# Delta rounds: the key scale folded into other operations, POOL's scaling of keys taken out

## The chip, the cores and the metric

One core of a Trainium2 chip runs the whole program in one launch. The time is device microseconds from start to end. Five engines matter: TensorE (PE in the profile, its weight loads PEld), VectorE (DVE), ScalarE (ACT), GpSimd (POOL), and SyncE (SP), which issues most transfers. Each engine works through its own instructions in order; they meet only through semaphores. All data are 32-bit floats.

## What is computed

The program is a stack of four blocks on an input of 4 x 512 x 512: a gated scan, a mixture of experts, a gated delta rule with 16 heads of 128, and a second mixture. The change touches only the delta rule, whose inner step is, in the reference:

```python
q = silu(q).reshape(B, S, NH, D)
k = silu(k).reshape(B, S, NH, D) * D ** (-0.5)
v = silu(v).reshape(B, S, NH, D)
def step(St, inp):
    q_, k_, v_, a_, b_ = inp
    sk = einsum('bhij,bhj->bhi', St, k_)
    err = sk - v_
    Sn = a_[..., None, None] * St - b_[..., None, None] * err[..., None] * k_[..., None, :]
    o_ = einsum('bhij,bhj->bhi', Sn, q_)
    return (Sn, o_)
```

After it the output is normalised per head, scaled by `ln_w`, shifted by `ln_b` and multiplied by a gate, `sigmoid(x @ Wg)`.

## The kernel before, in words

`phase_delta` handles 16 rounds (`NR`), one for each pair of a group of four heads and a sequence of 512 tokens. Round 0 and round 15 are written apart; rounds 1 to 14 are a loop of seven passes with two rounds in each. A round has four chunks (`TPB`) of 128 tokens. The recurrence over a chunk is turned into matrices: `kk` = k k^T, `kq` = k q^T, a decay matrix `G`, `negL` = -kk * G, whose unit triangular inverse `R` is needed, and `A` = kq * G. After the inverses come four sequential steps in which the state `S` goes from chunk to chunk.

Each round `r` also prepares round `r + 1`: twelve projections ("units": k 0 to 3, q 4 to 7, v 8 to 11), each a matmul on PE (L1564), a first tap on ACT (L1776), three more taps on DVE (L1929) and a SiLU on ACT (L1781). Units share the two PSUM banks `pj`, so that unit u + 2 can only be projected once DVE has done the taps of unit u (L1562); unit 7 has a bank of its own.

The orders are written out by hand, one for each engine.

- **POOL** (L1519 to L1532): the masks `masked_la` and `masked_b` of chunks 1 to 3 (L1487, L1491); then `scale_keys` (L1493), four instructions for the four heads of the next round's keys, each of which waits for the SiLU of that head; then `finish_gates` (L1505), which turns tanh into sigmoid on this round's four gate chunks; then `gate_out` (L1507), twelve instructions that apply `ln_w`, `ln_b` and the gate to the output of round r - 1, chunk by chunk (L1517); last `copy_tables` and the masks of chunk 0 for the next round.
- **DVE** (L2010): for each chunk `G`, `negL`, `A`, `kd` (L2016 to L2024) and taps of a unit; then `diagonal_inverse` (L1932), which inverts the 32 x 32 diagonal blocks in 31 steps, each a product `block_t` (L1946) and a sum `block_X` (L1950), both `tensor_tensor` with both inputs and the output in SBUF and each waiting for the one before it. Taps of unit 3 stand before step 24 and those of unit 4 before step 27. Two transposes follow (L1952, L1954), then taps of units 5 and 6.
- **ACT** (L1802): tanh of the gate chunks (L1768), with the SiLUs of keys 0 to 2 and the normalisation of the previous output's chunks 0 to 2 (L1797) between them; then the first taps of units 3 and 4, the SiLU of key 3, the first tap of unit 5, the normalisation of chunk 3; then it waits for the first transpose and spreads the blocks into `T` and `R` (L1848).
- **PE** (L1588): the round begins with a wait for `k_scaled` (L1598). After the chunk matrices come the gate projections (L1577), units 3 to 6 and the first half of unit 7, then `z_blocks` (L1645), which waits for the spread `T`, the second half of unit 7, `r_blocks` (L1659), further steps of the inverse, and the state steps with units 8 to 11 between them. The turned-out output of round r - 1 (L1585) waits for `gate_out`.

Of the kernel before, what the change touches and what calls it, by code (L numbers as in the profile page):

```python
# [19 lines left out]
P = 128  # L20
# [20 lines left out]
DH = 128  # L41
HG = 4
# [8 lines left out]
class Program:  # L51
# [8 lines left out]
    def sem(self, name):  # L60

        self.phase_sems.append(self.nc.alloc_semaphore(name=name))
        return self.phase_sems[-1]
# [55 lines left out]
def stand(e, passed):  # L119

    e.sem_inc(passed, 1)
# [1166 lines left out]
def phase_delta(pr, con, tab):  # L1288
# [3 lines left out]
    H4 = [P, HG, P]  # L1292
    NR = NG * NB
    TAP_STEPS = TAPS - 1
    CONVS = 3 * HG
    NL = len(LEVELS)
    NM = TPB * HG
# [5 lines left out]
    with ExitStack() as st:  # L1303
        sb = lambda n, s: pr.sb(st, "c_" + n, s)
        ps = lambda n, s: pr.ps(st, "c_ps_" + n, s)
        sem = lambda n: pr.sem("c_" + n)
# [4 lines left out]
        heads = [{m: sb(f"{m}T{i}", [P, HG, SEQ]) for m in "kq"} for i in range(2)]  # L1311
# [5 lines left out]
        beta, log_decay, before, upto, whole = (sb(k, [P, TPB, HG]) for k in ("beta", "log_decay", "before", "upto", "whole"))  # L1317
        masked_la, masked_b = sb("masked_la", [P, HG, P]), sb("masked_b", [P, HG, P])
        G = sb("G", [P, 2, HG, P])
        negL = sb("negL", [P, TPB, HG, P])  # L1320
        A = sb("A", [P, TPB, HG, P])
        R, T = sb("R", [P, TPB, HG, P]), sb("T", [P, TPB, HG, P])
        Z = sb("Z", [P, TPB, HG, P])
        kd = sb("kd", [P, TPB - 1, HG, DH])
# [19 lines left out]
        kk, kq, d4, z4, r4, t4 = (by_head(x) for x in (kk_ps, kq_ps, d_ps, z_ps, r_ps, t_ps))  # L1344
# [20 lines left out]
        tables = sem("tables")  # L1365
# [1 line left out]
        tap_done = sem("tap_done")  # L1367
        conv_step = sem("conv_step")
        silu_done = sem("silu_done")
        k_scaled = sem("k_scaled")  # L1370
        g_copied, g_done = sem("g_copied"), sem("g_done")
        la_masked, b_masked = sem("la_masked"), sem("b_masked")
        d_ready, decay_done, G_done = sem("d_ready"), sem("decay_done"), sem("G_done")
        kk_ready, L_done, A_done = sem("kk_ready"), sem("L_done"), sem("A_done")
# [4 lines left out]
        kt_ready, kd_done, vt_ready, v_done = sem("kt_ready"), sem("kd_done"), sem("vt_ready"), sem("v_done")  # L1379
# [28 lines left out]
        def _(e):  # L1408
# [21 lines left out]
            for r in range(NR):  # L1430
# [6 lines left out]
                if r + 2 < NR:  # L1437
                    e.wait_ge(gp_ready, TPB * r + TPB)
                    e.wait_ge(conv_step, TAP_STEPS * (CONVS * (r + 1) + 2))
                    load_round(r + 2)  # L1440
# [9 lines left out]
        @block.gpsimd  # L1450
        def _(e):
            for s, k in ((conv_step, 2 * TAP_STEPS), (silu_done, 4), (ot_done, 2), (ot_stored, 16)):
                e.sem_inc(s, k)

            made = 0
            e.affine_select(out=upper_of[:, :], in_=con["ones"][:, 0:TPB], compare_op=ALU.is_ge, fill=0.0, base=-BH,
                            pattern=[[-BB, TPB]], channel_multiplier=1).then_inc(masks_made, 1)
            made += 1
            e.memset(flat_L, 0.0).then_inc(masks_made, 1)
            made += 1  # L1460
            e.wait_ge(masks_made, made)
            e.affine_select(out=upper_of[:, :], in_=upper_of[:, :], compare_op=ALU.is_gt, fill=0.0, base=BB,
                            pattern=[[BB, TPB]], channel_multiplier=-1).then_inc(masks_made, 1)
            for i in range(2):
                e.affine_select(out=one_of[i], in_=one_of[i], compare_op=ALU.not_equal, fill=1.0, base=-i,
                                pattern=[[1, BB], [-2, BH]], channel_multiplier=0).then_inc(masks_made, 1)
            made += 3
            e.wait_ge(masks_made, made)
            for a in (negL, Z, T, R):
                e.memset(a[:, :, :, :], 0.0).then_inc(cleared, 1)  # L1470
            e.wait_ge(cleared, 4)
            e.wait_ge(ln_loaded, 32)

            def copy_tables(r):

                for dst, name in ((beta, "beta"), (log_decay, "log_decay"), (before, "decay_before"),
                                  (upto, "decay_upto"), (whole, "decay_all")):
                    src = tab[name][:, :, :, :, :].rearrange("p g b c h -> p (g b) c h")
                    e.tensor_copy(dst[:, :, :].unsqueeze(1), src[:, bass.ds(r, 1)]).then_inc(tables, 1)
                e.wait_ge(tables, 5 * r + 5)  # L1480
                stand(e, pr.waits_passed)

            def mask_gates(r, c):
                if c > 0:
                    e.wait_ge(d_ready, r * TPB + c)
                    stand(e, pr.waits_passed)
                e.tensor_tensor(masked_la[:, :, :], on_heads(log_decay, c), over_heads(con["upto"]), ALU.mult).then_inc(la_masked, 1)  # L1487
                if c > 0:
                    e.wait_ge(G_done, r * TPB + c)
                    stand(e, pr.waits_passed)  # L1490
                e.tensor_tensor(masked_b[:, :, :], on_heads(beta, c), over_heads(con["upto"]), ALU.mult).then_inc(b_masked, 1)  # L1491

            def scale_keys(q, buf):  # L1493

                for h in range(HG):
                    e.wait_ge(silu_done, CONVS * q + h + 5)
                    stand(e, pr.waits_passed)
                    e.tensor_scalar(heads[buf]["k"][:, h, :], heads[buf]["k"][:, h, :], DH ** -0.5, None, ALU.mult).then_inc(k_scaled, 1)  # L1498

            def finish_gates(r, buf):  # L1500

                for c in range(TPB):
                    e.wait_ge(g_copied, r * TPB + c + 1)
                    stand(e, pr.waits_passed)
                    e.tensor_scalar(gates[buf][:, c], gates[buf][:, c], 0.5, 0.5, ALU.mult, ALU.add).then_inc(g_done, 1)  # L1505

            def gate_out(q, buf, c):  # L1507

                n = q * TPB + c
                e.wait_ge(o_normed, HG * n + HG)  # L1510
                e.wait_ge(g_done, n + 1)
                stand(e, pr.waits_passed)
                for i, (b, op) in enumerate(((over_heads(ln_w), ALU.mult), (over_heads(ln_b), ALU.add), (gates[buf][:, c], ALU.mult))):
                    if i > 0:
                        e.wait_ge(o_gated, 3 * n + i)
                        stand(e, pr.waits_passed)
                    e.tensor_tensor(o[:, c], o[:, c], b, op).then_inc(o_gated, 1)  # L1517

            def a_round(r, buf, last=False):  # L1519
                for c in range(1, TPB):  # L1520
                    mask_gates(r, c)
                if not last:
                    scale_keys(r + 1, 1 - buf)
                finish_gates(r, buf)
                if after_first(r):
                    for c in range(TPB):
                        gate_out(r - 1, 1 - buf, c)
                if not last:
                    e.wait_ge(qS_done, (r + 1) * (TPB - 1))
                    stand(e, pr.waits_passed)  # L1530
                    copy_tables(r + 1)
                    mask_gates(r + 1, 0)  # L1532

            def first():
                copy_tables(0)
                mask_gates(0, 0)
                scale_keys(0, 0)

            def tail(r, buf):
                a_round(r, buf, last=True)  # L1540
                for c in range(TPB):
                    gate_out(r, buf, c)

            rounds(e, first, lambda r, buf, half: a_round(r, buf), tail)

        @block.tensor
        def _(e):
# [40 lines left out]
            def a_round(r, buf, half, last=False):  # L1588
# [6 lines left out]


                e.wait_ge(silu_done, CONVS * r + 2 * HG + 4)
                e.wait_ge(k_scaled, HG * r + HG)  # L1598
                for c in range(TPB):
                    n = r * TPB + c  # L1600
                    if c > 0:
# [306 lines left out]
        def _(e):  # L1908
# [101 lines left out]
            def a_round(r, buf, half, last=False):  # L2010
                next_taps = lambda u: None if last else taps(r + 1, 1 - buf, u, 16 * half + 16)
                for c in range(TPB):
                    n = r * TPB + c
                    e.wait_ge(decay_done, n + 1)
                    e.wait_ge(b_masked, n + 1)
                    e.tensor_tensor(G[:, c % 2], G[:, c % 2], masked_b[:, :, :], ALU.mult).then_inc(G_done, 1)  # L2016
                    e.wait_ge(G_done, n + 1)
                    e.wait_ge(kk_ready, n + 1)
                    e.scalar_tensor_tensor(negL[:, c, :, 1:P], kk[:, :, 1:P], -1.0, G[:, c % 2, :, 0:P - 1],  # L2019
                                           ALU.mult, ALU.mult).then_inc(L_done, 1)  # L2020
                    e.tensor_tensor(A[:, c], kq, G[:, c % 2], ALU.mult).then_inc(A_done, 1)  # L2021
                    if c < TPB - 1:
                        e.wait_ge(kt_ready, r * (TPB - 1) + c + 1)
                        e.tensor_tensor(kd[:, c], r4, G[:, c % 2, :, P - 1:P].to_broadcast(H4), ALU.mult).then_inc(kd_done, 1)  # L2024
                    if after_first(r):
                        norm_part(r - 1, c)
                    if c < TPB - 1:
                        next_taps(c)
# [48 lines left out]
            def tail(r, buf):  # L2077
                a_round(r, buf, None, last=True)
                for c in range(TPB):
                    norm_part(r, c)  # L2080

            rounds(e, first, a_round, tail)


# [362 lines left out]
```

## Time and profile before

| | us |
|---|---|
| median of 3 runs | 3600.45 |
| lowest and highest run | 3596.86, 3601.14 |
| the profiled execution, own time | 3595.2 |
| its span | 3593.6 |
| PE busy | 3054.6 (85%) |
| DVE busy | 1947.3 (54%) |
| ACT busy | 1177.0 (33%) |
| POOL busy | 742.8 (21%) |
| L1498 `scale_keys` on POOL, 64 instructions | 96.1 |
| L1517 `gate_out` on POOL, 192 instructions | 243.6 |
| L1946 and L1950 on DVE, 992 instructions | 347.3 |

A share of busy time is a mean over stages. The delta rounds are one stage of the program, and within a round the work of the engines is a chain, so a timeline of one round tells more than the table. The granted clock of PE is given as a fraction of full speed (1.00 is 2.4 GHz, 0.50 is 1.2 GHz; a value between is a mean over a stretch that has both).

### The profile page before, as it was taken

The page shows a single profiled execution, that of the slowest core. Times are in us where ns is not written, and L with a number is a line of the kernel's source. Part 1 is how long each engine was busy: PE and PEld are TensorE (multiplying, and loading weights), DVE is VectorE, ACT ScalarE, POOL GpSimd, SP SyncE. Part 2 cuts the span into 40 slices and gives each one's busy share as a digit, 9 for nine tenths or more (in the row PEclk, how much of TensorE's full clock was granted, in tenths as well). Part 3 has the DMA queues.
Part 4 walks back from the last instruction along what each step waited for, and adds up shares of the span by engine and source line. Part 5 has one row for each costly group of instructions (what it writes and reads, how often), then busy time and mean ns, then how long its engine had stood idle before and what let it go on. Part 6 is the DMA issues. An engine that isn't in the chain of part 4 may idle for free. (4 is left out here: it accounts for less than half of the span.)

```text
span 3593.6 us, 42797 instructions
## 1 busy us (share of the span) xinstructions
PE 3054.6 (85%) x13268; PEld 1746.6 (49%) x13269; DVE 1947.3 (54%) x4458; ACT 1177.0 (33%) x2104; POOL 742.8 (21%) x861
## 2 busy tenths in 40 slices
PE   7899889989991489999999999999999986599276
PEld 3344354446660346555665555665555654244122
DVE  5676710001114367777767778676777766045532
ACT  3555301011111133444444444434444433121122
POOL 1111022011113031333223232232332232200000
PEclk9999879999995599999999989999999987799688
DMA  2001240032215210011000110001000000532101
GB/s 106 24 12 36 78 183 24 12 119 67 66 58 195 92 73 13 25 45 40 25 13 25 48 37 25 17 21 56 35 19 25 13 13 12 234 105 82 41 35 47
DMA packets 66770, 196.86 MB, mean 55 GB/s; under 512 B 10512, under 2 KB 11168, under 8 KB 60192
## 3 DMA queue, kind: packets, MB, share of 16 engines
q1 hardware_dynamic: 43392, 133.67, 10.0%
q0 software_dynamic: 12256, 39.89, 3.5%
q10 hardware_dynamic: 10944, 21.02, 1.6%
q8 instruction: 100, 1.64, 0.2%
q14 instruction: 78, 0.64, 0.1%
HBM read 137.90 MB, written 56.66 MB: 54 GB/s over the span
## 5 line engine op out<-in xcount | busy, mean ns | idle before, releaser
L1929 DVE SCALAR_TENSOR_TENSOR c_conv<-c_ps_pj,c_conv_t,c_conv 128x511 f32<-128x511 f32 x528 | 393.7, 746 | 48.5 <-ACT c_conv L1776 35.9
L1564 PE MATMUL c_ps_pj<-c_xs,c_w_v 128*128 128x512 f32 x512 | 252.0, 619 | 0.0
L2140 PE MATMUL d_ps_yo<-d_w_o,d_heads 128*128 128x512 f32 x512 | 225.9, 604 | 24.4 <-DMA d_heads<-ot_d 24.4
L1564 PE MATMUL c_ps_pj<-c_xs,c_w_k 128*128 128x512 f32 x512 | 232.5, 598 | 10.8 <-DMA c_xs<-xt_d 10.8
L1577 PE MATMUL c_ps_pj<-c_w_g,c_xs 128*128 128x512 f32 x512 | 227.6, 592 | 0.0
L1564 PE MATMUL c_ps_pj<-c_xs,c_w_q 128*128 128x512 f32 x384 | 175.6, 601 | 24.5 <-DVE c_conv L1929 24.5
L1946 DVE TENSOR_TENSOR c_block_t<-c_block_L,c_block_X 128x126 f32<-128x126 f32 (+22 forms) x496 | 185.5, 374 | 16.0
L1776 ACT ACTIVATE c_conv<-c_ps_pj,c_conv_t 128x512 f32<-128x512 f32 x176 | 136.3, 774 | 148.1 <-PE c_ps_pj L1564 144.8
L2140 PEld LDWEIGHTS d_ps_yo<-d_w_o,d_heads 128*128 128x128 f32 x512 | 99.2, 194 | 149.4 <-issue 149.3
L1498 POOL TENSOR_SCALAR c_kT<-c_kT 128x512 f32<-128x512 f32 x64 | 96.1, 1501 | 364.7 <-ACT c_kT L1781 364.7
L1950 DVE TENSOR_TENSOR c_block_X<-c_block_X,c_block_t 128x126 f32<-128x126 f32 (+22 forms) x496 | 161.8, 326 | 17.0
L1577 PEld LDWEIGHTS c_ps_pj<-c_w_g,c_xs 128*128 128x128 f32 x512 | 94.8, 190 | 107.1 <-issue 107.1
L1564 PEld LDWEIGHTS c_ps_pj<-c_xs,c_w_k 128*128 128x128 f32 x512 | 93.5, 192 | 106.5 <-issue 93.7
L1113 DVE TENSOR_TENSOR x_act<-x_hs,x_ps_u 128x352 f32<-128x352 f32 x40 | 20.8, 521 | 226.9 <-ACT x_hs L1098 226.9
L1564 PEld LDWEIGHTS c_ps_pj<-c_xs,c_w_v 128*128 128x128 f32 x512 | 94.1, 204 | 72.4 <-issue 70.7
L966 DVE TENSOR_TENSOR b_act<-b_hs,b_ps_u 128x512 f32<-128x512 f32 (+1 forms) x24 | 16.5, 686 | 206.3 <-PE b_ps_u L858 206.3
L357 POOL TENSOR_SCALAR a_skip<-a_xc,a_col_d 128x512 f32<-128x512 f32 x32 | 62.5, 1953 | 314.9 <-ACT a_xc L471 172.8
L1564 PEld LDWEIGHTS c_ps_pj<-c_xs,c_w_q 128*128 128x128 f32 x384 | 69.1, 190 | 120.0 <-issue 69.6
L1606 PE MATMUL c_ps_kk<-c_kT 128*128 128x128 f32 x512 | 103.2, 284 | 27.7 <-DVE c_A L2021 25.0
L1064 PE MATMUL x_ps_g<-b_w_gu,x_xT 128*128 x320 | 122.7, 466 | 1.4 <-ACT x_xT L1089 0.8
L1824 ACT ACTIVATE c_err<-c_negL 32x128 f32<-32x128 f32 x256 | 78.6, 307 | 137.6 <-DVE c_negL L2019 132.8
L377 PE MATMUL a_ps_pj<-XT,a_w_in 128*128 128x512 f32 x256 | 119.8, 612 | 3.5 <-DVE a_conv L602 2.7
(363 smaller groups left out, 6219.6 us busy)
## 6 DMA issues: line engine op xcount, KB each, us to landing
c_xs<-xt_d SPq DMA_DIRECT2D x16, 1024.0 KB, 4.9
ot_d<-c_oT ACTq DMA_DIRECT2D x64, 256.0 KB, 2.0
d_heads<-ot_d POOLq DMA_DIRECT2D x16, 1024.0 KB, 6.6
b_w_gu<-in_w_gu SPq DMA_DIRECT2D x8, 1408.0 KB, 25.2
y_slots<-x_y SPq DMA_DIRECT2D x40, 256.0 KB, 2.0
a_x<-in_x SPq DMA_DIRECT2D x8, 1024.0 KB, 6.5
x_w_dn<-in_w_dn SPq DMA_DIRECT2D x8, 768.0 KB, 11.0
x<-a_x SPq DMA_DIRECT2D x4, 1024.0 KB, 4.3
```

The costliest lines, as they stand in the source:

```text
L377: mm = e.matmul(pj[c % 2][:, :], w_in[:, k, c * P:(c + 1) * P], XT[:, b, k, :], start=(k == 0), stop=(k == KD - 1))
L1064: e.matmul(g_ps[par][:, 0:FE], xT[par][:, k, :], w_gu[:, expert, k, 0:FE], start=(k == 0), stop=(k == KD - 1))
L1498: e.tensor_scalar(heads[buf]["k"][:, h, :], heads[buf]["k"][:, h, :], DH ** -0.5, None, ALU.mult).then_inc(k_scaled, 1)
L1564: mm = e.matmul(bank_of[u][:, :], w["kqv"[u // HG]][:, k, (u % HG) * DH:(u % HG + 1) * DH], xs[xb][:, k, :], start=(k == 0), stop=(k == KD ...
L1577: mm = e.matmul(pj[1 - i % 2][:, :], xs[xb][:, k, i * P:(i + 1) * P], w["g"][:, k, :], start=(k == 0), stop=(k == KD - 1))
L1606: e.matmul(kk[:, h, :], chunk(kT, h, c), chunk(kT, h, c), start=True, stop=True)
L1776: e.activation(conv[:, u % 4, :], bank_of[u][:, :], ACT.Identity, bias=conv_t[buf][:, m, h, TAPS:TAPS + 1], scale=conv_t[buf][:, m, h, TAP ...
L1824: e.activation(corners[on_q, c, :, :], negL[on_q, c, :, on_q], ACT.Copy).then_inc(corner_cut, 1)
L1929: e.scalar_tensor_tensor(oc, bank_of[u][:, 0:SEQ - s], conv_t[buf][:, m, h, TAPS - 1 - s:TAPS - s], oc, ALU.mult, ALU.add).then_inc(conv_s ...
L1946: e.tensor_tensor(t, block_L[:, i + 1:BB, i].unsqueeze(2).to_broadcast([P, n, k]), block_X[:, i, 0:k].unsqueeze(1).to_broadcast([P, n, k]) ...
L1950: e.tensor_tensor(below, below, t, ALU.add).then_inc(sub_step, 1)
L2140: mm = e.matmul(yo[c % 2][:, :], heads[:, c, h, :], w_o[:, h, :], start=(h == 0), stop=(h == NH - 1))
```

## The change

The keys are left unscaled after their SiLU. The factor, 128 ** -0.5, moves to where keys are used: squared into `negL` (k k^T), once into `A` and into `kd`, and into the table `before`, by which the product of keys and state is multiplied. Two DVE instructions become `scalar_tensor_tensor` instead of `tensor_tensor`; POOL loses four instructions a round with their waits, and gains one on 128 x 16 elements with a wait behind it; PE loses one wait.

```diff
+    KEY_SCALE = DH ** -0.5
...
-                e.wait_ge(tables, 5 * r + 5)
+                e.wait_ge(tables, 6 * r + 5)
+                stand(e, pr.waits_passed)
+                e.tensor_scalar(before[:, :, :], before[:, :, :], KEY_SCALE, None, ALU.mult).then_inc(tables, 1)
+                e.wait_ge(tables, 6 * r + 6)
                 stand(e, pr.waits_passed)
...
-            def scale_keys(q, buf):
-
-                for h in range(HG):
-                    e.wait_ge(silu_done, CONVS * q + h + 5)
-                    stand(e, pr.waits_passed)
-                    e.tensor_scalar(heads[buf]["k"][:, h, :], heads[buf]["k"][:, h, :], DH ** -0.5, None, ALU.mult).then_inc(k_scaled, 1)
-
...
             def a_round(r, buf, last=False):
                 for c in range(1, TPB):
                     mask_gates(r, c)
-                if not last:
-                    scale_keys(r + 1, 1 - buf)
                 finish_gates(r, buf)
...
             def first():
                 copy_tables(0)
                 mask_gates(0, 0)
-                scale_keys(0, 0)
...
-                e.wait_ge(k_scaled, HG * r + HG)
...
-                    e.scalar_tensor_tensor(negL[:, c, :, 1:P], kk[:, :, 1:P], -1.0, G[:, c % 2, :, 0:P - 1],
+                    e.scalar_tensor_tensor(negL[:, c, :, 1:P], kk[:, :, 1:P], -KEY_SCALE * KEY_SCALE, G[:, c % 2, :, 0:P - 1],
                                            ALU.mult, ALU.mult).then_inc(L_done, 1)
-                    e.tensor_tensor(A[:, c], kq, G[:, c % 2], ALU.mult).then_inc(A_done, 1)
+                    e.scalar_tensor_tensor(A[:, c], kq, KEY_SCALE, G[:, c % 2], ALU.mult, ALU.mult).then_inc(A_done, 1)
...
-                        e.tensor_tensor(kd[:, c], r4, G[:, c % 2, :, P - 1:P].to_broadcast(H4), ALU.mult).then_inc(kd_done, 1)
+                        e.scalar_tensor_tensor(kd[:, c], r4, KEY_SCALE, G[:, c % 2, :, P - 1:P].to_broadcast(H4), ALU.mult, ALU.mult).then_inc(kd_done, 1)
```

## Rows read from the trace of the kernel before

**Rows 1.** Busy time by stretch, the delta rounds: us, busy of each engine, PE clock.

```profile
1283.00:3117.00 1834.00, 1640.95 (x9412) 1035.78 (x9411) 1296.06 (x3130) 773.96 (x1453) 518.24 (x524) 0.91 0.09 31
```

**Rows 2.** Waits of the delta rounds: us in total, times, longest.

```profile
ACT c_T L1848 <- DVE c_block_L L1952: 94.2, 16, 18.4
...
PE c_ps_z L1645 <- ACT c_T L1848: 67.8, 15, 22.7
```

**Rows 3.** Timeline of DVE, one middle round (columns: start us, duration us).

```profile
1884.31 0.21 DVE L1946 TENSOR_TENSOR c_block_t<-c_block_L,c_block_X 128x31 f32<-128x31 f32 x1
...
1885.54 0.58 DVE L1950 TENSOR_TENSOR c_block_X<-c_block_X,c_block_t 128x58 f32<-128x58 f32 x1
...
1894.37 0.29 DVE L1950 TENSOR_TENSOR c_block_X<-c_block_X,c_block_t 128x128 f32<-128x128 f32 x1
...
1899.65 2.31 DVE L1929 SCALAR_TENSOR_TENSOR c_conv<-c_ps_pj,c_conv_t,c_conv 128x511 f32<-128x511 f32 x3
...
1903.70 2.31 DVE L1929 SCALAR_TENSOR_TENSOR c_conv<-c_ps_pj,c_conv_t,c_conv 128x511 f32<-128x511 f32 x3
...
1906.85 1.20 DVE L1946 TENSOR_TENSOR c_block_t<-c_block_L,c_block_X 128x45 f32<-128x45 f32 x1
...
1912.16 1.10 DVE L1952 STREAM_TRANSPOSE c_block_L<-c_block_X 128x512 f32<-128x512 f32 x1
```

**Rows 4.** Timeline of PE, the same round.

```profile
1902.02 3.70 PE L1564 MATMUL c_ps_pj<-c_xs,c_w_q 128*128 128x512 f32 x8 [1.16 <-DVE c_conv L1929]
...
1909.60 1.88 PE L1564 MATMUL c_ps_kq<-c_xs,c_w_q 128*128 128x512 f32 x4
1914.71 0.18 PE L1645 MATMUL c_ps_z<-c_T,c_negL 32*32 32x32 f32 x1 [3.23 <-ACT c_T L1848]
...
1915.99 3.46 PE L1564 MATMUL c_ps_kq<-c_xs,c_w_q 128*128 128x512 f32 x4
```

**Rows 5.** Timeline of POOL, the same round.

```profile
1885.43 1.49 POOL L1498 TENSOR_SCALAR c_kT<-c_kT 128x512 f32<-128x512 f32 x1 [10.46 <-ACT c_kT L1781]
...
1904.39 2.36 POOL L1505 TENSOR_SCALAR c_gate<-c_gate 128x512 f32<-128x512 f32 x4
1906.72 1.27 POOL L1517 TENSOR_TENSOR c_o<-c_o,c_ln_w 128x512 f32<-128x512 f32 x1
...
1921.95 1.26 POOL L1517 TENSOR_TENSOR c_o<-c_o,c_gate 128x512 f32<-128x512 f32 x1 [0.18 <-POOL c_o L1517]
```

**Rows 6.** Timeline of ACT, the same round.

```profile
1893.15 0.60 ACT L1768 ACTIVATE c_gate<-c_ps_pj 128x512 f32<-128x512 f32 x1 [0.74 <-PE c_ps_pj L1577]
...
1906.43 1.64 ACT L1797 ACTIVATE c_o<-c_o,c_o_nb,c_o_rs 128x128 f32<-128x128 f32 x4
1913.29 1.28 ACT L1848 ACTIVATE c_T<-c_block_L 32x512 f32<-32x512 f32 x2 [5.22 <-DVE c_block_L L1952]
```

**Rows 7.** Timeline of POOL, the last round, which has no `scale_keys`.

```profile
2990.26 1.29 POOL L1517 TENSOR_TENSOR c_o<-c_o,c_ln_w 128x512 f32<-128x512 f32 x1
...
3003.10 1.29 POOL L1517 TENSOR_TENSOR c_o<-c_o,c_ln_w 128x512 f32<-128x512 f32 x1
```

**Rows 8.** Timeline of DVE, the last round.

```profile
2990.46 1.25 DVE L1946 TENSOR_TENSOR c_block_t<-c_block_L,c_block_X 128x135 f32<-128x135 f32 x1
...
3003.30 1.22 DVE L1946 TENSOR_TENSOR c_block_t<-c_block_L,c_block_X 128x108 f32<-128x108 f32 x1
...
3010.83 1.06 DVE L1952 STREAM_TRANSPOSE c_block_L<-c_block_X 128x512 f32<-128x512 f32 x1
```

**Rows 9.** Busy time by stretch, one of each round, columns as in rows 1.

```profile
1914.70:1919.30 4.60, 4.59 (x68) 2.39 (x68) 3.71 (x5) 4.43 (x8) 4.24 (x5) 0.63 0.01 4
...
2990.00:3000.00 10.00, 0.66 (x4) 0.42 (x4) 9.72 (x9) 3.50 (x9) 9.27 (x8) 0.71 0.00 1
```

**Rows 10.** Groups by line and shape, DVE: times, busy us, mean ns.

```profile
L2019 DVE SCALAR_TENSOR_TENSOR c_negL<-c_ps_kk,c_G 128x508 f32<-128x508 f32 x64 | 43.9, 686 | 2.2
L2021 DVE TENSOR_TENSOR c_A<-c_ps_kq,c_G 128x512 f32<-128x512 f32 x64 | 43.5, 680 | 0.0
```

More of the change, by code:

```diff
@@ L1369, in phase_delta @@
         silu_done = sem("silu_done")
-        k_scaled = sem("k_scaled")
         g_copied, g_done = sem("g_copied"), sem("g_done")
```

## The prediction

> **What bounds the kernel now.** I read the busy times by stretch first. The delta rounds take 1834 us of the span, with PE busy for 1641 of them [rows 1], so what a round costs is set mostly by how seldom PE waits. Next the waits of that stretch: PE waits 15 times, 67.8 us in all, at `z_blocks` for the spread `T`, and ACT waits 16 times, 94.2 us in all, for DVE's transpose before it can spread [rows 2]. So in every round there is one place where the chain leaves PE: DVE's `diagonal_inverse`, then ACT, then PE at L1645. Everything of the round behind `z_blocks` stands behind it in PE's order, the next round's first matmuls too; a shift of `z_blocks` has nothing to be absorbed in. The timelines of one middle round show the same place: PE ends its work for the next round, idles 3.23 us, and starts `z_blocks` at 1914.71 [rows 4], 1.4 us after ACT began to spread at 1913.29 [rows 6], which DVE's transpose of 1912.16 had released [rows 3].
>
> **Where POOL stands in it.** POOL is busy for only 518 us of 1834 [rows 1] and never on the chain. But look at what DVE's small instructions last. They take 0.2 to 0.3 us: from 1894.37 to 1899.65 DVE does 17 of them, 0.31 us each. At 1885.54 one takes 0.58, while POOL's key scaling of 1885.43 runs; at 1906.85 one of 45 elements takes 1.20, while POOL's first `gate_out` instruction (1906.72, 1.27 us) runs [rows 3, 5]. A `gate_out` instruction thus holds such a DVE instruction for nearly its whole length, a key scaling for about 0.3 us. The taps (L1929, one input in PSUM) keep their 2.31 for three, and the transposes their length.
>
> **What the change moves.** `scale_keys` for head 3 waits for the SiLU of unit 3, behind DVE's taps of 1899.65 to 1901.96. Until then POOL's queue stands still, and `finish_gates` and `gate_out` wait behind it: the gates are finished at 1904.39 and `gate_out` starts at 1906.72 [rows 5], when DVE has 8 small instructions left; it holds four of them. Without `scale_keys`, nothing of that wait is left. The last gate chunk leaves ACT at 1893.15 + 0.60 = 1893.75 [rows 6]; three gates are finished by then, the fourth takes 2.36 / 4 = 0.6 [rows 5], and `gate_out` starts at about 1894.5, when DVE has 17 instructions to go before the taps of unit 3, and 14 behind them.
>
> **What that costs is in the trace already**, since the last round has no `scale_keys`. There `gate_out` starts at 2990.26, its tenth instruction at 3003.10 [rows 7]. DVE does 12 small instructions from 2990.46 to 3003.30 [rows 8], 12.84 us, 1.07 each in place of 0.31.
>
> **The sum for a middle round**, in the times of the round shown:
> - Chunks 0 to 2 of `gate_out`, nine instructions, run from 1894.5 to 1907.3 (12.84 as in the last round). DVE does 12 of its 17. Chunk 3 can't follow: its normalisation on ACT stands behind the first tap of unit 5.
> - The other 5 at 0.31 end at 1908.9: taps of unit 3 start there, not at 1899.65, 9.2 late. They end at 1911.2.
> - Six instructions at 0.25, 1.5: taps of unit 4 from 1912.7 to 1915.0. Eight at 0.24, 1.9, now unheld: the transpose starts at 1916.9 instead of 1912.16 [rows 3]. DVE is **4.7 us** later.
> - PE: unit 5 waits for the taps of unit 3 and starts at 1911.2 instead of 1902.02. PE has then been idle since 1900.9. In the last round PE did nearly nothing from 2990.7 on and the granted clock of 2990 to 3000 was 0.71, that is the 2.4 GHz level first and 1.2 GHz for the last 5.8 us; in the middle round 1914.7 to 1919.3 had 0.63 [rows 9], and four matmuls that had taken 1.88 took 3.46 [rows 4]. So I charge unit 5 the same 1.6 for a low clock: 5.3 instead of 3.7, to 1916.5. Unit 6 (3.5, as from 1906.1 to 1909.6) to 1920.0, the first half of unit 7 (1.7) to 1921.7. `T` is spread by then. `z_blocks` starts at 1921.7 instead of 1914.71, **7.0 us** later: PE's own queue has become later than DVE's chain.
> - One thing comes back. PE has been busy for 10 us by then, so the second half of unit 7 should take 1.88, not 3.46 [rows 4]: 1.6 us. Left over: **5.4 us** a round.
>
> If the clock does not fall, unit 5 takes 3.7, unit 6 waits for its taps until 1915.0, and the round loses 5.6 - 1.6 = 4.0; if unit 5 runs wholly at 1.2 GHz, 7.4, it loses 7.5. I take 5.4, between: the stretch of the last round says that the clock does fall beside such idling, and the row of 3.46 that one such piece of work costs 1.6.
>
> This holds for rounds 1 to 14. Round 0 has no `gate_out`; round 15 is as before. 14 x 5.4 = **76 us**.
>
> **The rest, costed small.** `A` and `kd` become the form of `negL`, 686 ns against 680 [rows 10]: seven a round, 0.04 us, lower end nothing, upper end 0.07 each as for a tap (2.31 / 3 = 0.77 less 0.68, on 16 rounds x 7: 10 us). I take the lower, for `negL` has the same operands. The new instruction on `before` and the wait behind it delay the first masks of the next round. No row of it is shown; it lies between nothing and one gate instruction (0.59 [rows 5]) plus the 0.18 of a wait on POOL itself [rows 5], and is hidden: POOL has been idle since 1923 and PE needs the mask only after its first eight matmuls of the round. If that cover were gone, it would be 0.8 x 15 = 12 us. PE's wait for `k_scaled` goes for nothing: the scalings were done 50 us earlier. The keys' scaling held three or four DVE instructions by 0.3 us each; in its place the gates' finishing now falls among DVE's small instructions and holds as many. I cost the pair at nothing (between a gain of 1.2 and a loss of 0.4 a round).
>
> The Trainium skill, SBUF — State Buffer, "Who interferes with whom", states a rule that speaks against this kind of move: a VectorE instruction with two SBUF inputs contends with a GpSimd instruction that reads SBUF, and whichever starts first holds the pair for its whole instruction. For `gate_out` the rows agree (1.20 beside 1.27). For `scale_keys` they don't: it lasts 1.49 and DVE's neighbour grew by 0.3.
>
> **Against which time.** The profiled execution took 3595.2; 76 more is 3671. The median of the runs shown is 3600.45, 5.2 higher, so the forecast is **3676 us**.
>
> **Rivals.**
> - *The clock does worse* (slower by more): the low level outlasts unit 5 and catches unit 6 as well, 7.5 + 3.5 = 11 a round, 154 us, 3754. For it: PE's idling grows from 1.2 to 10 us at this place. Against: in the middle round 1914.7 to 1919.3 has 0.63 and not 0.50, so the level came back while PE worked. 8%.
> - *Faster*: POOL's relief wins. It needs `gate_out` to stay clear of DVE's small instructions, that is, to start when fewer than about five of them are left, or the taps to fall into it. Then the four 0.3 us holds of the scaling and some of the four 1 us holds of today go: 1.2 to 4 us x 14, 17 to 56 us, 3583 at the near end. Its point of decision is the start of the first `gate_out`: after 1906 it would be right. Against: only `finish_gates` stands before it, and its last input is there at 1893.75. 5%.
> - *No change*: the delay of DVE is hidden, as PE's 3.23 us of idling would hide one if it were on another chain; 3600. Against: that idling is itself the wait for this chain [rows 4, 6]. 4%.
> - *The skill's rule for every GpSimd instruction*: if a key scaling also held DVE for its 1.49, the three that fall among small instructions would cost 4.5 a round now and not 0.9, and taking them out would give 3.6 back. 5.4 - 3.6 = 1.8 a round, 25 us, 3625. The 0.58 of [rows 3] speaks against it. 2%.
> - The forecast has the remaining 81%.
>
> **Range and chances.** Within the forecast, 4.0 to 7.5 a round is 56 to 105; one POOL instruction more or less among DVE's is 1.1 a round, so 3 to 7.5, 42 to 105: 3642 to 3706. About 0.2%, 7 us, is what a measurement of this kernel can tell from no change. Slower by more: 0.91; within: 0.04; faster: 0.05.
>
> **What would show it.** In the profile after: `gate_out` of chunk 0 about 12 us earlier in the round, in one run of nine with its last three apart; about nine of DVE's L1946 and L1950 at over 1 us in each middle round, not four, so that their total grows by some 14 x 4.7 = 66 us; taps of unit 3 some 9 us later; PE's wait for DVE at unit 5 grown from 1 to some 10 us, and its wait at `z_blocks` gone; a period of the round about 5 us longer. If instead the transposes come 4.7 late but PE's unit 5 is not late, the term of the queue is wrong; if DVE's small instructions keep their lengths, the whole forecast is.

## The result and the profile after

The changed kernel took 3686.41 us (median of 4; 3683.94 to 3689.04), the kernel before beside it 3598.65: ratio 1.0245, interval 1.0228 to 1.0263, **slower** by 88 us. Forecast: 3676, range 3642 to 3706.

The profiled execution has a span of 3687.4, 93.8 more than before's. From the start of round 1 to that of round 15 (ACT's first table load of each) it needs 1621.8 us in place of 1533.6, so 88.2 lie in the fourteen rounds, **6.3 a round**; the last round is unchanged, and 5.4 us lie ahead of the delta rounds, where nothing was changed and where executions differed by as much.

The same round as before, DVE (start, duration). It lies 28.86 us later in this profile (ACT's table load at 1884.69 against 1855.83 opens it):

```profile
1923.59 1.24 DVE L1942 TENSOR_TENSOR c_block_X<-c_block_X,c_block_t 128x128 f32<-128x128 f32 x1
1924.87 0.30 DVE L1938 TENSOR_TENSOR c_block_t<-c_block_L,c_block_X 128x135 f32<-128x135 f32 x1
1925.20 1.25 DVE L1942 TENSOR_TENSOR c_block_X<-c_block_X,c_block_t 128x135 f32<-128x135 f32 x1
1926.48 1.40 DVE L1938 TENSOR_TENSOR c_block_t<-c_block_L,c_block_X 128x126 f32<-128x126 f32 x1
...
1937.69 2.31 DVE L1921 SCALAR_TENSOR_TENSOR c_conv<-c_ps_pj,c_conv_t,c_conv 128x511 f32<-128x511 f32 x3
...
1945.53 1.09 DVE L1944 STREAM_TRANSPOSE c_block_L<-c_block_X 128x512 f32<-128x512 f32 x1
```

POOL beside it:

```profile
1922.80 0.62 POOL L1501 TENSOR_SCALAR c_gate<-c_gate 128x512 f32<-128x512 f32 x1 [3.25 <-ACT c_gate L1760]
1923.39 1.30 POOL L1513 TENSOR_TENSOR c_o<-c_o,c_ln_w 128x512 f32<-128x512 f32 x1
1924.86 1.43 POOL L1513 TENSOR_TENSOR c_o<-c_o,c_ln_b 128x512 f32<-128x512 f32 x1 [0.18 <-POOL c_o L1513]
...
1948.58 1.27 POOL L1513 TENSOR_TENSOR c_o<-c_o,c_ln_w 128x512 f32<-128x512 f32 x1 [12.13 <-ACT c_o L1789]
```

The small instructions that took 0.3 us now take 1.2 to 1.4 beside `gate_out`; there are nine such in this round. Some pass at their old length: the one of 1924.87 took 0.30 although POOL's next instruction had begun at 1924.86, and it is POOL's that is longer then, 1.43 in place of 1.27. In all, 13 small instructions take 13.0 us beside the nine of POOL, from 1923.59 to 1936.61. Less the 28.86, `gate_out` starts at 1894.53, the taps of unit 3 at 1908.83, those of unit 4 at 1912.60, the transpose at 1916.67: 4.51 later than in [rows 3]. PE and its waits:

```profile
1940.06 9.35 PE L1557 MATMUL c_ps_pj<-c_xs,c_w_q 128*128 128x512 f32 x16 [10.33 <-DVE c_conv L1921]
...
1951.06 0.21 PE L1637 MATMUL c_ps_z<-c_T,c_negL 32*32 32x32 f32 x1
...
1952.19 1.98 PE L1557 MATMUL c_ps_kq<-c_xs,c_w_q 128*128 128x512 f32 x4
...
1957.12 0.68 PE L1665 MATMUL c_ps_t<-ident,c_R 64*128 64x64 f32 x8 [1.81 <-ACT c_R L1858]
```

```profile
PE c_ps_pj L1557 <- DVE c_conv L1921: 149.7, 15, 11.0
PE c_ps_t L1665 <- ACT c_R L1858: 27.3, 15, 1.9
...
PE c_ps_z L1637 <- ACT c_T L1840: 22.7, 1, 22.7
```

The wait at `z_blocks` [rows 2] is left in the last round alone; in its place PE waits 10 us a round ahead of unit 5. Units 5 and 6 then take 9.35 together, where at a full clock the same sixteen matmuls take 7.46 (run 8). The clock, third column from the end, says why:

```profile
1929.50:1940.10 10.60, 0.27 (x2) 0.04 (x1) 10.17 (x15) 0.84 (x2) 6.41 (x5) 0.73 0.00 0
1940.10:1949.40 9.30, 9.30 (x17) 4.09 (x18) 8.68 (x22) 4.41 (x9) 0.82 (x1) 0.76 0.00 0
```

Over the whole kernel (line, busy us, mean ns), DVE's 992 small instructions grew from 347.3 to 411.8, that is by 64.5; the folded forms cost nothing, as beside [rows 10]:

```profile
L1938 DVE TENSOR_TENSOR c_block_t<-c_block_L,c_block_X 128x126 f32<-128x126 f32 (+22 forms) x496 | 206.6, 417 | 16.0
L1942 DVE TENSOR_TENSOR c_block_X<-c_block_X,c_block_t 128x126 f32<-128x126 f32 (+22 forms) x496 | 205.2, 414 | 17.0
...
L2013 DVE SCALAR_TENSOR_TENSOR c_A<-c_ps_kq,c_G 128x512 f32<-128x512 f32 x64 | 43.6, 681 | 0.0
```

### The profile page after: what moved, and what is told of

Read it like the earlier page. It is cut to its first block and busy times, and to the rows that moved or that the text cites. A ratio compares the mean times of both kernels' runs of the same rounds, so it can differ in the third digit from the quotient of the medians.

```text
span 3687.4 us, 42657 instructions
## 1 busy us (share of the span) xinstructions
PE 3054.3 (83%) x13268; PEld 1744.2 (47%) x13269; DVE 2012.3 (55%) x4458; ACT 1175.2 (32%) x2104; POOL 662.1 (18%) x813
## 5 line engine op out<-in xcount | busy, mean ns | idle before, releaser
L1557 PE MATMUL c_ps_pj<-c_xs,c_w_q 128*128 128x512 f32 x384 | 206.6, 696 | 149.7 <-DVE c_conv L1921 149.7
L1557 PE MATMUL c_ps_pj<-c_xs,c_w_k 128*128 128x512 f32 x512 | 232.1, 597 | 10.9 <-DMA c_xs<-xt_d 10.9
L1938 DVE TENSOR_TENSOR c_block_t<-c_block_L,c_block_X 128x126 f32<-128x126 f32 (+22 forms) x496 | 206.6, 417 | 16.0
L1942 DVE TENSOR_TENSOR c_block_X<-c_block_X,c_block_t 128x126 f32<-128x126 f32 (+22 forms) x496 | 205.2, 414 | 17.0
L1557 PEld LDWEIGHTS c_ps_pj<-c_xs,c_w_q 128*128 128x128 f32 x384 | 83.5, 226 | 261.9 <-DVE c_conv L1921 164.1
L1513 POOL TENSOR_TENSOR c_o<-c_o,c_ln_w 128x512 f32<-128x512 f32 x64 | 83.0, 1297 | 230.7 <-ACT c_o L1789 230.7
L1065 PE MATMUL x_ps_u<-b_w_gu,x_xT 128*128 x320 | 121.9, 463 | 0.0
```

Source lines behind the costliest of these rows:

```text
L1065: mm = e.matmul(u_ps[par][:, 0:FE], xT[par][:, k, :], w_gu[:, expert, k, FE:2 * FE], start=(k == 0), stop=(k == KD - 1))
L1557: mm = e.matmul(bank_of[u][:, :], w["kqv"[u // HG]][:, k, (u % HG) * DH:(u % HG + 1) * DH], xs[xb][:, k, :], start=(k == 0), stop=(k == KD ...
L1938: e.tensor_tensor(t, block_L[:, i + 1:BB, i].unsqueeze(2).to_broadcast([P, n, k]), block_X[:, i, 0:k].unsqueeze(1).to_broadcast([P, n, k]) ...
L1942: e.tensor_tensor(below, below, t, ALU.add).then_inc(sub_step, 1)
```

## The experiments

The theory: the loss is `gate_out`'s new place, among DVE's small instructions, and what PE's queue and clock add to it. Its rivals are these: the folded forms and the new table instruction cost it; any POOL work there would cost it, not only that with two inputs; the clock is not on the path. Each ratio is to the kernel before on the same chip (3595.92 for runs 1 to 4; 3594.01 for 6, 7, 9 and 10; 3595.04 for 5, 8 and 11). Differences from the changed kernel use its 3686.41, and those between runs of the two groups also go across chips. `stand`, in some cuts, only counts a wait in a semaphore that nobody waits for.

**1. `hold_queue`: the old order, no scaling.**

```diff
+                if not last:
+                    e.wait_ge(silu_done, CONVS * (r + 1) + HG + 4)
+                    stand(e, pr.waits_passed)
                 finish_gates(r, buf)
```

> The changed kernel, but POOL waits for the SiLU of the next round's fourth key before it finishes the gates, as the removed scaling made it do; it scales nothing. Theory 1 (the loss is gate_out's place among DVE's small instructions): within 15 us of the kernel before, 3585 to 3610, with gate_out about 1.5 us earlier in the round than there. Theory 2 (the loss is in the folded forms, the new instruction on the table and its wait): as the changed kernel, 3680 to 3690.

Measured: 3584.3, ratio 0.9968 (0.9957 to 0.998). One wait gives back the 88 us and 12 more. `gate_out` starts 1.7 us earlier in the round than in the kernel before (49.2 against 50.9 after the table load) and holds four small instructions, as there. The removal of the scaling itself is a small gain, 0.8 us a round by the medians; the wait that it had held was worth 102 us, some nine times that. Between the profiled executions, rounds 1 to 14 are 10.6 us shorter than in the kernel before, but only 3.9 shorter than in `fold_only`, whose profile lacks the two long rounds that are spoken of below. The gain is thus 0.3 to 0.8 us a round.

**2. `fold_only`: the folded forms in the kernel before.**

```diff
-                e.wait_ge(tables, 5 * r + 5)
+                e.wait_ge(tables, 6 * r + 5)
+                stand(e, pr.waits_passed)
+                e.tensor_scalar(before[:, :, :], before[:, :, :], 1.0, None, ALU.mult).then_inc(tables, 1)
+                e.wait_ge(tables, 6 * r + 6)
...
-                    e.tensor_tensor(A[:, c], kq, G[:, c % 2], ALU.mult).then_inc(A_done, 1)
+                    e.scalar_tensor_tensor(A[:, c], kq, 1.0, G[:, c % 2], ALU.mult, ALU.mult).then_inc(A_done, 1)
```

(`kd` likewise.) 

> The kernel before with the folded forms alone, all their factors 1.0 (A and kd as scalar_tensor_tensor, the extra multiplication of the table with its wait); the keys are scaled by POOL as before. Theory 1: 0 to 12 us over the kernel before, 3598 to 3610, the lower end if the forms cost 6 ns as negL does. Theory 2: most of the 88 us, over 3660.

Measured: 3594.97, ratio 0.9999 (0.9987 to 1.0012): nothing. The table's instruction takes 277 ns in its profile; only POOL's own next mask waits for it, 3.7 us in all sixteen rounds.

**3. `one_input_gate_out`: the same place, one input each.**

```diff
-                    e.tensor_tensor(o[:, c], o[:, c], b, op).then_inc(o_gated, 1)
+                    e.tensor_scalar(o[:, c], o[:, c], 1.0, None, ALU.mult).then_inc(o_gated, 1)
```

> The changed kernel with each of gate_out's twelve instructions replaced by a multiplication of the output by 1.0, one input in place of two (ln_w, ln_b and the gate are left out of the result). Such an instruction took 1.49 us as key scaling. Theory 1a (a POOL instruction with two inputs holds DVE's for its length, one with one input for 0.3 us): nine holds of 0.3 = 2.7 us a round instead of 9, so 3575 to 3610. Theory 1b (any POOL instruction holds DVE for its length): 1.49 against 1.27 and 12 of them, 3690 to 3730.

Measured: 3573.45, ratio 0.9944 (0.9925 to 0.9962), just under the first range and far from the second. A row of POOL and one of DVE beside it:

```profile
1889.66 1.49 POOL L1513 TENSOR_SCALAR c_o<-c_o 128x512 f32<-128x512 f32 x1 [0.19 <-POOL c_o L1513]
```

```profile
1889.76 0.65 DVE L1942 TENSOR_TENSOR c_block_X<-c_block_X,c_block_t 128x126 f32<-128x126 f32 x1
```

POOL is busy longer than with `gate_out`, in the same place, yet no small instruction of DVE in rounds 1 to 14 takes over 0.71 us. In the round shown at most one beside each of POOL's takes 0.5 to 0.7, and the others their normal time. So it is not the presence or the length of POOL's work that costs, but its kind. Whether the second input alone makes the difference is not shown: the edit goes from `tensor_tensor` to `tensor_scalar` and from two inputs to one at once, and no run has the one without the other. The Trainium skill (SBUF — State Buffer, "Who interferes with whom") makes no such difference among GpSimd instructions that read SBUF; here the measurement decides.

**4. `gate_out_late`: `gate_out` behind DVE's inverse.**

```diff
                 if after_first(r):
+                    e.wait_ge(T_turned, r + 1)
+                    stand(e, pr.waits_passed)
                     for c in range(TPB):
                         gate_out(r - 1, 1 - buf, c)
```

> The changed kernel, but POOL starts gate_out only when DVE's diagonal inverse is through its first two transposes. Theory 1: no small instruction of DVE is held by gate_out; the transpose comes some 4 us earlier in the round than in the kernel before, z_blocks 3 to 4 us earlier, PE being the next limit: 3540 to 3560, faster than both kernels. Theory 2: 3680 or so. A third (gate_out late makes PE wait for the turned-out output instead): 3600 or more, with PE's wait for L1517's output grown.

Measured: 3527.8, ratio 0.9816 (0.9799 to 0.9834), below both kernels and 12 under my range. No small instruction of rounds 1 to 14 is over 0.70 us, and the transpose comes 4.2 us earlier in an even round than in the kernel before, `z_blocks` 3.1. The third theory is out: in rounds 1 to 14 PE never waits for `gate_out`. The 12 us under the range are the last round's: I had counted the middle rounds only, and it had twelve holds too ([rows 8] show the first of them), so that from its start to the end of the program is now 631.2 us, not 641.8.

**5. `late_without_the_fold`: the same wait in the kernel before**, keys scaled by POOL.

> The kernel before, keys scaled by POOL, with nothing but the wait for DVE's first two transposes ahead of gate_out. If the place of gate_out is what decides and the scaling's own holds are 0.3 us each, this is within 15 us of gate_out_late: 3525 to 3545. If the scaling itself was worth much once gate_out is out of the way: 3550 or more.

Measured: 3525.53, ratio 0.9812 (0.9792 to 0.9833). With `gate_out` late, the scaling of keys costs nothing that can be told.

**6. `one_chunk_early`: chunk 0 early, the rest late** (the wait of experiment 4 ahead of chunk 1).

> The changed kernel, but only chunk 0 of gate_out may run among DVE's small instructions; chunks 1 to 3 wait for the first two transposes. If each of gate_out's instructions costs its length less the one DVE instruction it lets pass, three of them cost 12.84 / 12 x 3 less 3 or 4 times 0.31, about 3 us a round over the version where all twelve are late (if that gives 3540 to 3560, this gives 3585 to 3605). If the loss of the changed kernel is made elsewhere (the queue of PE, its clock), this differs from the late version by less than 15 us.

Measured: 3594.78, ratio 0.9998 (0.9988 to 1.0008): 67 over the late version, 4.8 a round and not 3, so the expectation was short by 1.8 a round. (That the time lies in the range named, 3585 to 3605, is luck: two errors, this one and the late version's, cancel.) DVE did as the rule says, its transpose is 3.0 and 3.3 later in two neighbouring rounds. The rest is PE's:

```profile
1906.73 9.34 PE L1560 MATMUL c_ps_pj<-c_xs,c_w_q 128*128 128x512 f32 x16 [4.51 <-DVE c_conv L1924]
```

After 4.5 us of idling units 5 and 6 take 9.34; in the same round of the late version, where PE idled for 1.50 ahead of them, they take 7.46. That is 1.9 us, and 3.0 or 3.3 and 1.9 make the 4.8.

**7. `pe_kept_busy`, and 8. `pe_busy_to_the_end`: matmuls of no use in PE's idle time.** The second, in the first `range(11)` is two times four:

```diff
                 for u in range(HG, 2 * HG - 1):
+                    if u == HG + 1 and not last:
+                        e.wait_ge(A_done, TPB * (r + 1))
+                        for i in range(11):
+                            k = i % KD
+                            e.matmul(kq_ps[:, :], w["q"][:, k, 0:DH], xs[1 - buf][:, k, :], start=(k == 0), stop=(k == KD - 1 or i == 10))
                     next_unit(u)
```

> The changed kernel with 32 instructions' worth of idle matmuls (two units, 7.2 us, into a bank that is free then) put on PE between units 4 and 5, where it idles 10 us. If the low clock of unit 5 is part of the loss, units 5 and 6 take 7.3 us in place of 9.35 and z_blocks comes 1 to 1.7 us earlier: 14 to 24 us less than the changed kernel, 3662 to 3672. If the clock is not on the path, 3682 to 3690; if the added work delays unit 5, more than that.

Measured: 3688.46, ratio 1.0259 (1.0241 to 1.0276). It could not decide: the added work ended 3.7 us before unit 5, and the clock fell all the same. In the round looked at it was 1.00 until unit 5 began and 0.66 from 1939.4 to 1944.4; units 5 and 6 took 8.8 there and 10.2 in the next round. Rounds 1 to 14 are 3.4 us shorter than in the changed kernel and round 0, to which the matmuls were added too, is 3.4 longer.

> As pe_kept_busy, but with 11 matmuls of 0.9 us in place of 8, so that PE is busy from the end of unit 4 until DVE's taps of unit 3 are nearly done and the clock has no cause to fall there (with 8 it fell all the same, 3 us before unit 5). If the low clock of units 5 and 6 is on the path: the two take 7.3 us in place of 9.3, z_blocks comes 1.5 to 2 us earlier, 3658 to 3672. If z_blocks comes earlier and the time stays (3680 or more), the stretch behind z_blocks, its own low clock or ACT, takes the gain back.

Measured: 3669.89, ratio 1.0213 (1.0188 to 1.0238). PE on both sides of the wait, and units 5 and 6:

```profile
1925.20:1935.50 10.30, 9.39 (x22) 3.80 (x20) 9.89 (x15) 0.77 (x2) 6.18 (x5) 1.00 0.00 0
1935.50:1942.90 7.40, 7.33 (x17) 3.15 (x18) 6.85 (x20) 4.18 (x9) 1.08 (x1) 1.00 0.01 2
```

```profile
1935.51 7.46 PE L1557 MATMUL c_ps_pj<-c_xs,c_w_q 128*128 128x512 f32 x16 [0.93 <-DVE c_conv L1926]
```

More work on PE, and rounds 1 to 14 are 27.3 us shorter than in the changed kernel (1594.5 against 1621.8), 1.95 each, while DVE's times are as they were (taps of unit 3 at 50.9 in an even round and the transpose at 58.8, within 0.05 in both). Round 0, where PE had no such idle time to fill, pays 7.2 of it back. The 1.95 are what the low clock ahead of `z_blocks` costs the changed kernel. They are not its net share of the loss, since the kernel before has a stretch of low clock behind `z_blocks` [rows 4, 9], and what went there came back.

**9. `act_order`: ACT's copy ahead.**

```diff
-                next_silu(HG)
-                next_tap(HG + 3)
                 e.wait_ge(rl_ready, 4 * r + 2)
                 e.activation(R[even_of[1], :, :, odd_of[1]], r_block[1][even_of[1]], ACT.Copy).then_inc(rb_done, 1)
+                next_silu(HG)
+                next_tap(HG + 3)
```

> The changed kernel with ACT's copy of the second r-block (L1858) put ahead of the SiLU of unit 4 and the first tap of unit 7, 1.4 us of ACT's time. If the 1.6 us that I expected back from the second half of unit 7 was lost to ACT's own chain between z_blocks and turn_inverse, PE's next step comes 0.7 to 1.4 us earlier: 10 to 20 us less, 3666 to 3677. If not, 3682 to 3690.

Measured: 3678.82, ratio 1.0237 (1.022 to 1.0254), against 1.0245 (1.0228 to 1.0263) for the changed kernel: the two can't be told apart. The step itself came: PE's wait for ACT at L1665 is gone, its place taken by one for DVE of 14.7 us in all, and from `z_blocks` to the turned blocks it takes 5.2 us, not 6.1. In the even round looked at the turned blocks even stand 2.2 us earlier (68.9 against 71.1 after its table load), but 1.3 of that is `z_blocks`: units 5 and 6, which the edit doesn't touch, took 8.8 there and not 10.1. Yet two neighbouring rounds take 232.1 together in both kernels. The odd one now has a granted clock of 0.91 in its first 20 us, where it was 1.00, and its `z_blocks` comes 2.4 later; what was won in one place was spent there.

**10. `late_and_act_order`** (4 and 9 together).

> gate_out late, as in the run before, and ACT's copy ahead, both together. If both work and are of different stretches of the chain: the late version less 10 to 20 us, 3525 to 3545. If the second half of unit 7 at the low clock is then the bound, as it was in the kernel before, the second gives nothing: within 5 us of the late version.

Measured: 3506.36, ratio 0.9756 (0.974 to 0.9772), 21 less than the late version. As a difference that is the end of the 10 to 20 expected; the range named in us is missed by 19, since it went by the time that I had expected of the late version. From `z_blocks` to the turned blocks it takes 5.2 and not 6.1, as in run 9, and here the rounds are shorter with it: rounds 1 to 14 take 1455.5 in place of 1472.0, 1.2 each.

**11. `gates_last`: the gates behind `gate_out` as well**, so that POOL is silent through the whole inverse. Against run 10:

```diff
-                finish_gates(r, buf)
                 if after_first(r):
                     e.wait_ge(T_turned, r + 1)
                     stand(e, pr.waits_passed)
                     for c in range(TPB):
                         gate_out(r - 1, 1 - buf, c)
+                finish_gates(r, buf)
```

> As late_and_act_order, but the four gate instructions of POOL (one input, 0.3 us held each) run behind gate_out, so that none of POOL's work falls among DVE's small instructions. Unit 5 waits for DVE's taps of unit 3, which come 1.2 to 1.4 us earlier: 17 to 20 us less than late_and_act_order if all of it passes on, 3485 to 3495; no less than 3500 if PE is the bound there or the clock takes it back.

Measured: **3486.84**, ratio 0.9709 (0.9688 to 0.9731), the best, and as expected: 108 under the kernel before, 200 under the changed one.

```profile
L1944 DVE TENSOR_TENSOR c_block_X<-c_block_X,c_block_t 128x126 f32<-128x126 f32 (+22 forms) x496 | 127.8, 258 | 17.0
L1940 DVE TENSOR_TENSOR c_block_t<-c_block_L,c_block_X 128x126 f32<-128x126 f32 (+22 forms) x496 | 127.5, 257 | 16.0
```

255 us is what these 992 cost with POOL out of their way (none of rounds 1 to 14 takes over 0.30); 92 of before's 347 and 157 of after's 412 were holding.

## Why the prediction was right, and which terms were off

The direction, the mechanism and the range held: 88 against a forecast of 76. By its own steps:

- *When `gate_out` starts*: 1894.5 forecast, 1894.53 measured. Nine together, then three apart behind ACT: so it was.
- *DVE*: taps of unit 3 at 1908.9, measured 1908.8; taps of unit 4 1912.7 and 1912.6; transpose 4.7 later, measured 4.5. The last round of the kernel before had been the experiment in advance. Shown again by runs 1, 4 and 6. One reading was wrong and moved nothing: when `gate_out` started in the kernel before, DVE had six small instructions left and not 8 (it holds four of them, as was said); 8 is their number from the taps of unit 4 on.
- *Clock of PE*: charged 1.6 for unit 5. **Too small.** Units 5 and 6 were put at 5.3 and 3.5, 8.8 in all, and took 9.35 in this round and 10.1 in the next, where they take 7.46 and 7.54 at a full clock (run 8). So `z_blocks` is 7.5 us late in this round and 8.3 in the next (forecast 7.0). Run 8 prices the clock at 1.95 a round.
- *"One thing comes back", 1.6*: **too large.** The second half of unit 7 did take 1.98 in place of 3.46. But by then ACT's chain was what PE waited for (27.3 us in 15 waits), so the turned blocks are 6.7 and 6.5 late: 0.8 and 1.8 came back, 1.3 on average.
- So a middle round loses some 6.6 where I had 5.4. Over fourteen it is 6.3, since two of them lost only 4: in the kernel before rounds 3 and 7 took 112.5 and 112.7 us where the other odd ones took 109.6 to 109.8, and in the changed kernel they are like the others. The trace shows where: these two have a granted clock of 0.91 in their first 20 us, where round 5 has 1.00, the same sign as in experiment 9. The profile of `fold_only`, with the same orders, has no such round, so they come with the execution. What sets the clock there was not tested.
- *Fold costed at nothing*: right (run 2). *Key scaling against gates, costed at nothing*: right within 1 us a round (run 1 gives a gain of 0.3 to 0.8 for the scaling's absence with the old wait kept).
- So the 12 us between 76 and 88 are sizes and not the mechanism: 0.9 a round too little up to `z_blocks`, the clock mostly, and 0.3 too much for what comes back make 17 in fourteen rounds, less some 5 for the two long rounds.
- The rival on the other side had its condition right: had `gate_out` stayed behind, the change would have been faster. Run 1, 3584, is that case, at 0.8 us a round, beside the near end that was named (3583, 1.2 a round).

## What to carry to other kernels

Work taken off an engine that is not on the path can cost more than it saves, if a wait in it kept the engine's later work away from a neighbour; before an instruction with a wait is removed, look at where the work behind it will start, and beside what. Where DVE runs a chain of small instructions with two SBUF inputs, keep POOL's `tensor_tensor` out of that stretch by a wait on its end: here one such wait was worth 70 us, and 88 were lost for lack of one. A round of a loop that is written otherwise (here the last) shows in the trace of before what the change will do to the rest.

## What the runs showed of the hardware that was not expected

- A POOL `tensor_scalar` with one SBUF input, 1.49 us long, lengthens one small DVE instruction by some 0.35; a `tensor_tensor` with two, 1.27 long, lengthens it by 0.95 to 1.1. The length of POOL's instruction alone doesn't tell what it costs DVE. (That holds for DVE instructions of 0.2 to 0.3 us with two SBUF inputs.)
- POOL's `tensor_scalar` on 128 x 512 took 1.49 with one operation and 0.6 with two (L1505, multiply and add) [rows 5].
- Time won on PE does not always pass on: with a stretch of low clock in each round, a shorter chain can move it onto other work. Experiment 9 took 0.9 us out of PE's wait in each round, and a pair of rounds kept its 232.1 us. That the clock did it is read from the granted clock of the odd rounds, and no run was made to separate it.
